# Second attention: both layer norms applied on ACT, K copied on ACT, one Newton chain for both inverse roots, first additions moved

## What is computed

```python
x = x + attn_a(layernorm(x))      # 16 heads of 8, rotary, causal
x = x + ffn(layernorm(x))         # 64 experts, the 4 best of each token
x = x + attn_b(layernorm(x))      # one head, band of 64 keys; outside it every score is 0
x = x + ffn(layernorm(x))         # the same experts

def layernorm(x): return (x - mean(x)) / sqrt(var(x) + 1e-5)
def attn_b(x):
    q, k, v = x @ WQ, x @ WK, x @ WV
    score = q @ k.T / sqrt(128) * band          # zero outside the band, not -inf
    return softmax(score) @ v
def ffn(x):
    gate, expert = top_k(sigmoid(x @ expert_sel.T), 4)
    return sum(gate * relu(x @ keys[expert]) @ values[expert])
```

## Time and profile before

| | |
|---|---|
| Device time, median of 3 runs | 1129.41 us (1124.34 to 1130.1) |
| The profiled execution | 1120.72 us, of which its span 1119.0 us, 1.7 us around it |
| Second attention, rounds -1 to 8 | about 556 to 918 us of the span |
| Rounds 2 to 5, no expert steps | 679.2 to 794.0 us, 28.7 us a round |
| Busy over the span | PE 802.9 us (72%), DVE 752.1 (67%), POOL 729.7 (65%), ACT 559.8 (50%) |
| Mean granted PE clock | 0.86 of 2.4 GHz |

### The profile page before, as it was taken

The page is one execution under the profiler, slowest core; times in us unless marked ns, Lnnn a source line. Parts: engine busy times, 40 slices in busy tenths (PEclk is TensorE's granted clock), DMA queues, the critical chain, the costliest instruction groups (busy, mean ns, idle before and its releaser), DMA issues.

```text
span 1119.0 us, 22668 instructions
## 1 busy us (share of the span) xinstructions
PE 802.9 (72%) x7290; PEld 590.3 (53%) x7290; DVE 752.1 (67%) x2101; ACT 559.8 (50%) x1505; POOL 729.7 (65%) x860
## 2 busy tenths in 40 slices
PE   2799988787878877679789986566478776994000
PEld 0444444444434432669789875445468776993000
DVE  3687898988878842576566788898676773773111
ACT  1167766776747665456546544444436553662000
POOL 6344648898975758665676457777745246666776
PEclk9889999999969988889989996785689898997555
DMA  6455655543237223359868642111156566995222
GB/s 191 135 200 203 210 163 175 189 142 117 67 91 237 61 70 100 107 162 273 240 172 239 180 127 69 48 51 51 49 150 172 147 181 180 263 283 164 71 61 63
DMA packets 206548, 163.82 MB, mean 146 GB/s; under 512 B 15968, under 2 KB 191072, under 8 KB 206432
## 3 DMA queue, kind: packets, MB, share of 16 engines
q1 hardware_dynamic: 183968, 110.43, 34.5%
q0 software_dynamic: 16384, 33.59, 10.4%
q10 hardware_dynamic: 6080, 18.35, 4.4%
HBM read 78.94 MB, written 83.36 MB: 145 GB/s over the span
## 4 chain that ended last, share of the span: by engine, by line
PE 34%; DVE 19%; POOL 19%; issue 12%; DMA 10%; ACT 5%; ACTq 0%; POOLq 0%; DVEq 0%; SPq 0%
PE ps L786 5%; PE ps L687 5%; POOL sorted_rows L1742 4%; PE ps L795 4%; DMA v_aug<-result_rows,dest 3%; PE ps L646 3%; PE ps L775 3%; DMA x_scaled<-result_rows,dest 3%; POOL y_heads L1756 2%; ACT arena L993 2%; POOL arena L1788 2%; POOL x_scaled L1756 2%; DVE row_max L1226 2%; POOL xn L1763 1%; PE ps L734 1%
## 5 line engine op out<-in xcount | busy, mean ns | idle before, releaser
L993 ACT ACTIVATE arena<-ps 128x512 f32<-128x512 f32 x320 | 183.0, 598 | 74.9 <-PE ps L619 73.7
L1742 POOL DMA_INDIRECT sorted_rows<-v_aug,dest x144 | 143.5, 997 | 97.9 <-issue 33.4
L1425 DVE COPY arena<-ps 128x512 f32<-128x512 f32 x128 | 88.1, 689 | 98.7 <-PE ps L775 98.3
L786 PE MATMUL ps<-arena 128*128 128x128 f32 x1024 | 145.6, 288 | 10.4 <-DVE arena L1425 9.1
L646 PE MATMUL ps<-arena 64*128 64x128 bf16 (+3 forms) x576 | 129.9, 305 | 28.8 <-DMA arena<-k_parts 15.2
L1226 DVE TENSOR_REDUCE row_max<-ps 128x1 f32<-128x512 f32 (+1 forms) x192 | 126.8, 681 | 30.6 <-PE ps L666 29.6
L982 ACT COPY arena<-ps 128x512 f32<-128x512 f32 x128 | 74.9, 586 | 144.6 <-PE ps L795 142.3
L786 PEld LDWEIGHTS ps<-arena 128*128 128x128 f32 x1024 | 133.3, 203 | 13.8 <-DVE arena L1425 10.0
L795 PE MATMUL ps<-arena 128*128 x1024 | 138.7, 279 | 0.9 <-ACT arena L982 0.9
L1742 POOL DMA_INDIRECT sorted_rows<-x_scaled,dest x112 | 111.7, 997 | 36.2 <-issue 23.7
L619 PE MATMUL ps<-arena 64*128 64x512 bf16 (+3 forms) x512 | 124.4, 311 | 15.0 <-ACT arena L993 12.4
(11 more groups left out here) (219 smaller groups left out, 1683.4 us busy)
## 6 DMA issues: line engine op xcount, KB each, us to landing
arena<-sorted_rows SPq DMA_DIRECT2D x128, 256.0 KB, 3.9
result_rows<-arena SPq DMA_DIRECT2D x128, 256.0 KB, 2.8
sorted_rows<-arena ACTq DMA_DIRECT2D x16, 1024.0 KB, 5.1
arena<-q_parts SPq DMA_DIRECT2D x16, 512.0 KB, 3.9
arena<-k_parts SPq DMA_DIRECT2D x16, 512.0 KB, 5.0
q_parts<-parts SPq DMA_DIRECT2D x52, 128.0 KB, 2.8
k_parts<-parts SPq DMA_DIRECT2D x38, 128.0 KB, 2.9
sorted_rows<-v_aug,dest POOLq DMA_INDIRECT x144
```

Of the source, the lines that this page charges most:

```text
L786: mm = pe.matmul(ps[:, e_bank(2, layer, half, n), P * i:P * i + P], ktile[:, v, P * i:P * i + P], xtt[:, v, P * i:P * i + P], start=True, ...
L993: nc.scalar.activation(prob[:, grp % 2, pr % 2, PROB_AT[u]:PROB_AT[u] + T], ps[:, v % 2, :], ACT.Exp, scale=SCALE_A).then_inc(exp_done, 1)
L1742: g.indirect_dma_start(sorted_d[b // HALF][:, :], bass.IndirectOffsetOnAxis(dest[:, 16 * b + n:16 * b + n + 1], 0), scaled_rows(layer, b)[ ...
```

## The change

- ACT applies both norms in place of DVE: four `Identity` activations a sequence, scale = inverse root, bias = -mean times inverse root (`apply_norm`, names N3 and N2). N3, of r, stands first in ACT's round, ahead of E; N2, of nxt, stands behind place 6, ahead of XT's copy.
- ACT copies K, behind Q.
- On DVE both statistics stand behind the output: `score_out` for b, then `combined_stats` for nxt, then one Newton chain over [128, 2, 4] in place of two over [128, 4], and one more instruction for `negb`.
- XT moves behind place 6 on PE, Q and K behind place 7, V behind place 8, each one place later; RK keeps its place behind V.
- `choose` begins right behind place 4, with places 5 and 6 among its parts; the additions of sequence b+2, slice 0, stand ahead of place 4.
- The four additions of sequence 0 move from ahead of round -1 to behind its place 3 (four expert steps).

The diff, cut to its core:

```diff
 # PE, the order of a round
                 attend(it, "O")
                 beside(it, 5)
+                beside(it, 6)
                 attend(it, "XT")
-                beside(it, 6)
+                beside(it, 7)
                 attend(it, "Q", "K")
-                beside(it, 7)
+                beside(it, 8)
                 attend(it, "V")
-                beside(it, 8)
                 beside(it, 9)
                 attend(it, "RK")
 # PE, the waits of XT and NT
-                    pe.wait_ge(ln2, 13 * b + 13)
+                    pe.wait_ge(norm2, TT * b + TT)
-                    pe.wait_ge(ln3, 13 * b + 13)
+                    pe.wait_ge(norm3, TT * b + TT)
 # ACT
+            def apply_norm(i, b, dst, done):
+                for t in range(TT):
+                    nc.scalar.activation(dst[:, t, :], x[:, TT * b + t, :], ACT.Identity, bias=negb[:, i, t:t + 1],
+                                         scale=rsb[:, i, t:t + 1]).then_inc(done, 1)
+                if name == "N3":
+                    act.wait_ge(shifts, b + 2)
+                    act.wait_ge(scaled, 16 * (B + b - 1))
+                    apply_norm(1, b, xn1[:, b % 2], norm3)
+                if name == "N2":
+                    act.wait_ge(shifts, b + 1)
+                    apply_norm(0, b, xn0, norm2)
+                elif name == "K":
+                    nc.scalar.copy(kt[b % 2], o).then_inc(free, 1)
-                attend(it, "E")
+                attend(it, "N3", "E")
 ...
                 beside(it, 5)
-                attend(it, "XT")
                 beside(it, 6)
-                attend(it, "Q")
+                attend(it, "N2", "XT")
                 beside(it, 7)
+                attend(it, "Q", "K")
+                beside(it, 8)
                 attend(it, "V")
 # DVE, the chain
+            def inverse_roots(lo, hi):
+                rs, y, half = rsb[:, lo:hi, :], guess[:, lo:hi, :], slope[:, lo:hi, :]
 ...
+                dve.wait_ge(rstd_b, n + 1)
+                nc.vector.scalar_tensor_tensor(out=negb[:, lo:hi, :], in0=mvb[:, lo:hi, :, 0], scalar=-1.0, in1=rs,
+                                               op0=ALU.mult, op1=ALU.mult).then_inc(shifts, 1)
 # DVE, the order of a round
-            for c in range(TOPK):
-                add_rows(0, 0, c)
 ...
                 beside(b, 0)
-                if route:
-                    dve.wait_ge(scaled, 16 * (B + r - 1))
-                    finish(ln_apply(x[:, TT * r:TT * r + TT, :], mv1, rs1, xn1[:, r % 2], r, ln3, rstd3))
                 beside(b, 1)
                 beside(b, 2)
                 beside(b, 3)
-                if prepare:
-                    combined_stats(nxt)
+                if b < 0:
+                    for c in range(TOPK):
+                        add_rows(0, 0, c)
+                add_soon(b + 2, 0)
                 beside(b, 4)
-                if prepare:
...
-                add_soon(b + 2, 0)
-                beside(b, 5)
                 if route:
                     choice = choose(B + r, *evacuated("LG", r))
                     advance(choice, 3)
                 add_soon(b + 2, 1)
-                beside(b, 6)
+                beside(b, 5)
                 if route:
                     advance(choice, 4)
-                beside(b, 7)
+                beside(b, 6)
                 if attend:
                     score_out(b)
+                if prepare:
+                    combined_stats(nxt)
+                if attend or prepare:
+                    inverse_roots(0 if prepare else 1, 2 if attend else 1)
+                beside(b, 7)
                 if route:
                     finish(choice)
                 beside(b, 8)
-                if prepare:
-                    o, free = bank_take("K", nxt)
-                    nc.vector.tensor_copy(kt[nxt % 2], o).then_inc(free, 1)
                 add_soon(b + 2, 2)
                 beside(b, 9)
                 if prepare:
                     outside_sums(nxt)
                 beside(b, 10)
                 if route:
 ...
```

More of the change, by code:

```diff
@@ L265, in build @@
         mhalf = sb("minus_half", [P, TT])
-        guess = sb("root_guess", [P, TT])
-        slope = sb("root_slope", [P, TT])
+        mvb = sb("mv_b", [P, 2, TT, 2])
+        rsb = sb("rs_b", [P, 2, TT])
+        negb = sb("neg_mean_rs_b", [P, 2, TT])
+        guess = sb("root_guess", [P, 2, TT])
+        slope = sb("root_slope", [P, 2, TT])
         xnt = sb("xnt", [P, 2, T + 32])
@@ L403, in build @@
         ln3 = sem("ln3")
-        rstd2 = sem("rstd2")
-        rstd3 = sem("rstd3")
+        rstd_b = sem("rstd_b")
+        shifts = sem("shifts_b")
+        norm2 = sem("norm2")
+        norm3 = sem("norm3")
         root_seq = sem("root_seq")
@@ L1122, in attend @@
             def attend(it, *names):
-                offs = {name: off for _, name, off in BJOBS}
+                offs = {name: off for _, name, off in BJOBS} | {"N2": 1, "N3": -1}
                 for name in names:
@@ L1141, in _ @@
                 beside(it, 5)
-                attend(it, "XT")
                 beside(it, 6)
-                attend(it, "Q")
+                attend(it, "N2", "XT")
                 beside(it, 7)
+                attend(it, "Q", "K")
+                beside(it, 8)
                 attend(it, "V")
-                for place in (8, 9, 10):
-                    beside(it, place)
+                beside(it, 9)
+                beside(it, 10)
                 attend(it, "VO")
@@ L1165, in take, with ln_stats @@
                 dve.wait_ge(misc_ready, job[name, b] + 1)
-            def ln_stats(src, st, mv, rs, b, seq, each=13, applied=None):
+            def ln_stats(src, st, mv, rs, b, seq, applied):
                 for t in range(TT):
@@ L1172, in ln_stats @@
                         yield 0.6
-                dve.wait_ge(seq, each * b + 4)
-                if applied is not None and b:
+                dve.wait_ge(seq, 9 * b + 4)
+                if b:
                     dve.wait_ge(applied, TT * b)
@@ L1178, in ln_stats @@
                 yield 0.6
-                dve.wait_ge(seq, each * b + 8)
-                nc.vector.tensor_scalar(rs[:, :], mv[:, :, 1], EPS, None, ALU.add).then_inc(seq, 1)
+                dve.wait_ge(seq, 9 * b + 8)
+                nc.vector.tensor_scalar(rs, mv[:, :, 1], EPS, None, ALU.add).then_inc(seq, 1)
                 yield 0.3
-            def ln_apply(src, mv, rs, dst, b, seq, rstd):
-                dve.wait_ge(rstd, b + 1)
-                for t in range(TT):
-                    nc.vector.tensor_scalar(dst[:, t, :], src[:, t, :], mv[:, t, 0:1], rs[:, t:t + 1],
-                                            ALU.subtract, ALU.mult).then_inc(seq, 1)
-                    if t % 2:
-                        yield 0.7
@@ L1192, in _ @@
-            roots = count()
-            def inverse_root(rs, b, seq, rstd):
-                q = 3 * ROOT_STEPS * next(roots)
-                dve.wait_ge(seq, 13 * b + 9)
-                nc.vector.tensor_scalar(guess[:, :].bitcast(I32), rs[:, :].bitcast(I32), -0.5, ROOT_BITS,
-                                        ALU.mult, ALU.add).then_inc(root_seq, 1)
+            roots = count()
+            def inverse_roots(lo, hi):
+                n = next(roots)
+                q = 3 * ROOT_STEPS * n
+                rs, y, half = rsb[:, lo:hi, :], guess[:, lo:hi, :], slope[:, lo:hi, :]
+                nc.vector.tensor_scalar(y.bitcast(I32), rs.bitcast(I32), -0.5, ROOT_BITS, ALU.mult, ALU.add).then_inc(root_seq, 1)
@@ L1200, in inverse_root @@
                 for i in range(ROOT_STEPS):
                     dve.wait_ge(root_seq, q + 3 * i + 1)
-                    nc.vector.scalar_tensor_tensor(out=slope[:, :], in0=rs[:, :], scalar=-0.5, in1=guess[:, :],
-                                                   op0=ALU.mult, op1=ALU.mult).then_inc(root_seq, 1)
+                    nc.vector.scalar_tensor_tensor(out=half, in0=rs, scalar=-0.5, in1=y, op0=ALU.mult, op1=ALU.mult).then_inc(root_seq, 1)
                     dve.wait_ge(root_seq, q + 3 * i + 2)
-                    nc.vector.tensor_tensor(slope[:, :], slope[:, :], guess[:, :], ALU.mult).then_inc(root_seq, 1)
+                    nc.vector.tensor_tensor(half, half, y, ALU.mult).then_inc(root_seq, 1)
@@ L1206, in inverse_root @@
                     dve.wait_ge(root_seq, q + 3 * i + 3)
                     last = i == ROOT_STEPS - 1
-                    nc.vector.scalar_tensor_tensor(out=(rs if last else guess)[:, :], in0=slope[:, :], scalar=1.5, in1=guess[:, :],
-                                                   op0=ALU.add, op1=ALU.mult).then_inc(rstd if last else root_seq, 1)
+                    nc.vector.scalar_tensor_tensor(out=rs if last else y, in0=half, scalar=1.5, in1=y,
+                                                   op0=ALU.add, op1=ALU.mult).then_inc(rstd_b if last else root_seq, 1)
@@ L1605, in combined_stats @@
                 dve.wait_ge(added, added_count(0, b, TOPK - 1))
[L1606 to L1607 removed]
```

(4 more changed lines are left out.)

20 lines of the change are left out of this document (7 added, 13 removed).

## The result

The changed kernel takes 1174.03 us (median of 4 runs, 1172.89 to 1176.16), the kernel before beside it 1126.88 (1121.36 to 1130.1): a ratio of 1.0433, with a 95% interval of 1.0396 to 1.0471. It is slower by 4.3%.

A forecast was written before the change was run, and what follows sets the result against it. It took POOL to bound rounds 2 to 5. Terms: +18 (rounds -1 to 1), +23.6 (2 to 5), 6.9 absorbed and +3.6 in round 6, -1.5 each in 7 and 8: +35, 1164 us on the median; wanted range 1130 to 1185.

The forecast's parts named there:

- Rounds -1 to 1: Start of the kernel's rounds: later XT, idle PE and later Newton end cost +18 us together (8 to 24).
- the chain from XT to RK: Each of rounds 2 to 5: N2, XT, Q, K, V and RK in sequence, 9.05 us with N2 and hand-overs.
- rival 3: The clock: PE idles from O to XT, XT to RK at 1.2 GHz throughout, 1179 to 1188 us; chance 0.12.
- the round's upper bound, 38.0: Rounds 2 to 5: a round takes 38.0 us if O is late and K, V, RK run at the lower level.
- the forecast's 34.6: Rounds 2 to 5: a round takes 34.6 us where it was 28.7, bounds 31.7 to 38.0; four rounds +23.6.
- both stalls that it predicted on DVE: Rounds 2 to 5: DVE waits 4.5 us for the logits' exponential and some 5 us for RK at `positions`.
- In rounds 2 to 5 POOL is the bound and DVE has some slack: Kernel before, rounds 2 to 5: POOL's solid row of transfers sets the pace, though DVE is busy 101.3 of 114.8 us.
- 6.9 us absorbed in round 6: Round 6: its first copy stood 20.4 us in because POOL was late, now 13.5, so 6.9 us of lag vanish.
- a forecast of 32.7: Round 6, from its first copy to the round's end: 32.7 us where it took 29.1, +3.6.
- Rounds 7 and 8: Nothing is prepared there, RK isn't delayed and the norm leaves DVE ahead of NT: -1.5 us each.
- That DVE's relief counts (1): Whole kernel: faster by 12 us, 1117 us, if RK is ready when DVE comes to `positions`; chance 0.13.
- That POOL covers (2): No change, -1 to +4 us, about 1131, if rounds -1 to 1 lose nothing and rounds take the low bound; chance 0.13.

The follow-up runs named there:

- kernel with 54 transposes: Changed kernel with 54 transposes of the identity on PE ahead of XT's wait for the second norm in rounds 2 to 5: 1.0334 of the kernel before.
- 1.0325: Changed kernel with the one-hot on DVE ahead of the output's additions and the rank products on PE ahead of XT: 1.0325 of the kernel before.
- 1.0262: Kernel of 1.0325 with N3 also moved behind XT's copy in the round that makes it: 1.0262 of the kernel before.
- 1.0267: Kernel of 1.0262 with `positions` also begun ahead of the sums of strips (`outside_sums`): 1.0267 of the kernel before.
- experiment 4: Kernel before with ten more reductions a round on DVE ahead of `positions` in rounds 2 to 5, 24 us in all: 1.0204 of the kernel before.
- the split one: Changed kernel with the first norm's statistics and own Newton chain back at place 3, ACT applying that norm behind place 4: 0.9948 of the kernel before.
- the one with the order alone: Kernel before with XT behind O and expert steps a place forward, separate Newton chains, norms and K's copy left on DVE: 0.9965 of the kernel before.
- ACT's part alone: Kernel before with ACT applying both norms and copying K, two Newton chains, statistics and steps in their old places: 1.0006 of the kernel before.

## Why the prediction came out as it did

**The mechanism was right and is shown.** The chain that the prediction built is the one in the trace, and taking its first link away (XT waiting for both statistics) takes all of the loss away. Slower was forecast, for that reason, at +35 us; it was +47.2 by the medians and +52.5 between the profiled executions.

**Rounds -1 to 1: right to a microsecond.** Of the forecast's +18, +18.2 came (table). Of the 4.5 ahead of round 0, 3.1 are the additions' move. The path is the forecast one too: XT comes at 580.87 in round -1 (580.5), waits 8.36 us in round 0 (8.4), and `positions` begins 35.75 us into round 1 (35).

**Rounds 2 to 5: the step that failed is the price of the chain from XT to RK.** Round 3 against the forecast's times into the round: `choose` 6.6 (6.5), x += O 12.45 (12.1), the chain's end 19.0 (18.4), XT's start 20.9 (19.75), `positions` 29.8 (27.5), the next round 37.1 (34.6).

- N2 was sized by the sixteen activations of `scale`, 0.30 us apart. Those of N2 take 481 ns each on the average for 389 and stand 0.39 apart: 1.65 for 1.2 us in four. `scale` takes one operand a partition from SBUF, N2 two. With the hand-over it is 1.9 us from the chain's end to XT for 1.35.
- Q, K and V took 2.05, 1.91 and 1.71 us where 1.71, 1.10 and 1.10 were put: 5.1 us from Q's start to RK's for 3.9. The prediction let PE come back to the upper level behind Q; in this round it comes back only during V. It had this as rival 3 and as the round's upper bound, 38.0, of which the rounds (36.7, 37.1, 38.8, 36.8) came close. The kernel with 54 transposes takes 34.7 us a round. That this is the forecast's 34.6, and that the 10.3 us that the clock is worth there are about what the four rounds were missed by (10.6), is chance: the forecast had already put XT and Q at the lower level. Of the 2.5 us missed in round 3 the clock from Q to RK makes 1.2, N2 0.55, and x += O, the merged chain and the rest of the round, each a little later or longer, the remainder.

**The round is closed twice.** The prediction ended it with RK. The second chain, by `scale` and the logits, isn't in it, though both stalls that it predicted on DVE (4.5 us for the logits, 5 for RK) are there at 4.4 and 5.2. It didn't matter for the sum; it mattered for every cure that left the merged chain in (1.0325, 1.0262, 1.0267).

**"In rounds 2 to 5 POOL is the bound and DVE has some slack": wrong.** 24 us more on DVE showed in full there. Taking 7 us off DVE showed 1, because DVE then waited 6.4 us more for O and the logits. No wait in these rounds of the kernel before is put down to POOL, and the prediction's remark that DVE doesn't end the waits is wrong as well: PE's NT waits 22.7 us for the norm that DVE applies (experiment 4). The rounds are set by the order of DVE, PE and ACT; the solid row runs beside them and holds up the first copy of round 6. The sum didn't rest on slack in these rounds, so the error cost nothing. The term that did rest on POOL, 6.9 us absorbed in round 6, measured 7.0 in the changed kernel (20.2 to 13.2 us into the round) and 5.8 in the kernel with added work. From that copy to the round's end it took 33.6 us for a forecast of 32.7.

**Rounds 7 and 8: -3 forecast, +0.6 measured.** DVE's norm is gone there, and the time isn't shorter. PE's waits for DVE's first copies of a step, in before and in after, from the start of round 7 to the last group of scatters:

```profile
PE ps L775 <- DVE arena L1425: 3.2, 2, 2.6
```

```profile
PE ps L780 <- DVE arena L1441: 7.6, 3, 3.9
```

PE's wait for the norm fell from 3.7 to 2.4 us and the 4.0 that it waited for a one-hot are gone; in their place it waits 4.4 us more for DVE's first copies and 1.5 more for one of them ahead of a first product, so that its waits in this stretch stay at about 17 us in all. That the steps' shifted places cause it was not tried; no kernel here gained more than 0.8 us in these rounds (74.1 us in the split one, 73.6 in the one with the order alone).

**Rivals.** That DVE's relief counts (1): ACT's part alone says no. That POOL covers (2): its cover was there (5.8 to 7.0 us for 6.9), its conditions were not, since rounds -1 to 1 lost 18.2 us and a round took 37.3 for the low bound of 31.7. The clock (3): right as a mechanism, and worth 10 us. The rule of the Trainium skill that speaks for offloading from a saturated DVE ("Perfetto Trace Analysis", "Optimizing Scalar/DVE Operations") is neither borne out by the kernel with ACT's part alone nor harmful there.

## What to carry to other kernels

When two short chains are merged into one to save instructions, look at who waits for the earlier one: the merged chain ends when the later input is there, and everything that stands behind its first consumer in an in-order queue moves with it. A cure that moves one of those waiters shows the next chain of nearly the same length; undo the merge first. Price matmuls behind a new wait at the lower clock level until a row shows them at the upper one, and test cover by adding work and by reading who ends the waits, not by the other engine's solid row.

## What the runs showed of the hardware

- PE's level can fall between XT and Q: in round 3, behind 4.72 us of transposes and a wait of 3.78 us XT's four transposes took 0.68 us, the upper level, and behind 0.85 us more of waiting Q took 2.04, the lower. With 6.80 us of transposes and a wait of 1.85 us ahead of XT, Q took 1.10 behind the same 0.85.
- An activation of 128x128 on ACT takes 481 ns with scale and bias from SBUF, 389 with the scale alone. The two also differ in their function, Identity and Copy, which no run here holds apart. The Trainium skill ("ScalarE: Activation LUTs", "What ACT_TABLE_LOAD costs") gives about 93 ns for each operand a partition; the 92 ns here agree.
- The work ahead of the second attention is the same in all of these kernels, and yet its last relu starts anywhere from 547.40 to 555.65 us in the profiles. Differences of a few microseconds between two profiles are read from that row on, not from the span's start.
